# Folding the final weight into the experts' second weights, and weighing each expert's result where it is made

## The reference

```python
# x: 4096 tokens of 256 numbers; 8 experts, hidden size 512, 2 experts for each token
x = layernorm(x + attention(x))
gating = softmax(x @ Wg + bg)                       # 8 gates for each token
top = argsort(gating)[..., -2:]
h = silu((x @ W1[e] + b1[e]) * (x @ W3[e] + b3[e])) # for each expert e
expert = h @ W2[e] + b2[e]                          # 256 numbers
mixed = sum over the two chosen e of gating[e] * expert[e]
out = layernorm(x + mixed @ Wf + bf)
```

## Time and profile before

| | |
|---|---|
| median of 3 runs | 1953.55 us (1951.57 to 1959.17) |
| the profiled execution | 1948.98 us |
| its span in the trace | 1947.3 us |
| busy: PE / DVE / ACT / POOL | 89% / 65% / 45% / 19% of the span |
| granted TensorE clock, mean | 0.941 of full |
| moved by DMA | 155.30 MB, mean 80 GB/s |

### The profile page before, as it was taken

One profiled execution on the slowest core, in us unless ns is written; L12 is line 12 of the kernel. 1 busy time (PEld: TensorE's weight loads), 2 busy tenths in 40 slices (PEclk: granted clock), 3 DMA queues, 4 the chain that ended last, 5 costly groups with the idle time before them and its releaser, 6 DMA issues.

```text
span 1947.3 us, 28314 instructions
## 1 busy us (share of the span) xinstructions
PE 1737.1 (89%) x9130; PEld 920.4 (47%) x9131; DVE 1262.3 (65%) x2992; ACT 882.6 (45%) x1035; POOL 366.4 (19%) x478
## 2 busy tenths in 40 slices
...
GB/s 102 137 238 236 179 129 147 7 36 70 8 73 39 15 90 7 57 50 7 99 12 39 67 7 121 13 60 204 205 95 38 47 43 48 44 43 49 44 132 151
DMA packets 99497, 155.30 MB, mean 80 GB/s; under 512 B 10752, under 2 KB 60736, under 8 KB 99008
## 3 DMA queue, kind: packets, MB, share of 16 engines
...
## 4 chain that ended last, share of the span: by engine, by line
PE 70%; DVE 8%; ACT 7%; issue 6%; DMA 5%; POOL 2%; SPq 1%; another core or an unknown queue 0%; ACTq 0%; DVEq 0%; POOLq 0%
PE att_ps_s L884 22%; PE exp_ps_h L1564 13%; PE att_ps_o L903 12%; PE att_ps_m L862 10%; PE exp_ps_y L1582 6%; ACT att_probs L931 3%; DMA out_parts<-att_out_t 2%; PE pre_ps_q L311 2%; PE exp_ps_t L1572 2%; PE pre_ps_h L311 1%; DVE att_maxima L945 1%; DMA k_parts<-pre_waves 1%; PE exp_ps_x L1553 1%; POOL sorted_rows L1449 1%; DMA route_a_inv<-inv_rows 1%
## 5 line engine op out<-in xcount | busy, mean ns | idle before, releaser
L931 ACT ACTIVATE att_probs<-att_ps_s 128x1024 f32<-128x1024 f32 (+3 forms) x640 | 563.7, 895 | 484.4 <-PE att_ps_s L884 476.5
L884 PE MATMUL att_ps_s<-att_queries,att_keys 49*128 49x512 f32 (+3 forms) x2560 | 632.8, 561 | 20.9 <-ACT att_probs L931 11.4
L945 DVE TENSOR_REDUCE att_maxima<-att_ps_m 128x1 f32<-128x512 f32 x768 | 487.1, 684 | 153.6 <-PE att_ps_m L862 148.6
L862 PE MATMUL att_ps_m<-att_keys,att_queries 48*128 48x512 f32 (+3 forms) x1280 | 506.5, 605 | 24.1 <-DVE att_maxima L948 15.9
L862 PEld LDWEIGHTS att_ps_m<-att_keys,att_queries 48*128 48x128 f32 x1280 | 197.7, 193 | 315.8 <-DVE att_maxima L945 141.4
L884 PEld LDWEIGHTS att_ps_s<-att_queries,att_keys 49*128 49x128 f32 x2560 | 242.9, 191 | 127.3 <-ACT att_probs L931 85.4
L948 DVE CUSTOM_DVE_ANT_0 att_ps_m<-att_ps_m,att_future 128x128 f32<-128x128 f32 (+3 forms) x512 | 240.3, 514 | 73.4 <-PE att_ps_m L862 72.1
L903 PE MATMUL att_ps_o<-att_probs,att_values 128*32 128x512 f32 (+3 forms) x2560 | 269.3, 535 | 11.1 <-POOL att_probs L1034 11.1
L1564 PE MATMUL exp_ps_h<-keep_w,exp_rows_t 128*128 x568 | 257.4, 596 | 5.5 <-DVE exp_rows_t L1598 5.5
L1640 ACT ACTIVATE exp_hidden<-exp_product 128x512 f32<-128x512 f32 x71 | 44.8, 632 | 343.7 <-DVE exp_product L1623 343.7
L1034 POOL TENSOR_SCALAR_AFFINE_SELECT att_probs<-att_probs 128x512 f32<-128x512 f32 x128 | 81.1, 634 | 491.3 <-ACT att_probs L931 491.2
...
## 6 DMA issues: line engine op xcount, KB each, us to landing
...
```

The lines of the kernel that those rows point to most:

```text
L862: pe.matmul(take()[:, 0:width], queries[g % 2][half, c, r, P * q:P * q + P], keys[g % 2][half, k, r, 0:width], start=True, stop=True).then ...
L884: mm = pe.matmul(score_tile(unit, first, last)[:, e], keys[g % 2][half, k // TPC, r, P * (k % TPC):P * (k % TPC) + P].bitcast(F32), querie ...
L931: act.activation(probs[:, step % PROBS, DUO * r:DUO * r + DUO, first:last], score_tile(unit, first, last), ACT.Exp, scale=SCALE).then_inc( ...
L945: dve.tensor_reduce(to, buf[:, 0:width], AX.X, ALU.max).then_inc(s_mr, 1)
```

## The change

Since (g1 E1 + g2 E2) Wf = g1 (E1 Wf) + g2 (E2 Wf), the final weight can go into the experts' second weights. The kernel after does this:

1. In `route` the ten blocks of `bias2` (2) and `w2` (8), each 4 experts wide, are multiplied by Wf and put back in their place: PE transposes a block (`turn_weight`, 8 transposes, through the same `ps_n` as turn_x1), ACT copies it to `turned`, PE multiplies it by `wf` (`multiply_weight`, 8 matmuls of 256 columns into a new `ps_f`), ACT copies the product back (`keep_folded`). Four of these folds (`FOLDS_AMONG`) stand among the rounds of the chunks, six behind the last round.
2. `wf` is loaded in `route` (round 2). The `w2` blocks are loaded in rounds 1 to 4 and half of b1 in round 5. The other half of b1 has its place where `turned` lies, so SP waits for the last fold's multiplication before it loads it; SP's loads of the first sorted rows stand behind that.
3. A sorted row carries its two gates and the number of its first result row (260 numbers in place of 258). In `experts`, DVE finds the gate of a row in one more tiny instruction per tile, ACT multiplies each result by its gate (`weigh`), and POOL's scatter waits for that. The results of one token now lie in neighbouring rows.
4. `finish` has no mixing, transposing, copying or Wf: PE adds the two results of a token by multiplying each by the identity into the same PSUM tile (8 matmuls per chunk), and then come residual, statistics and norm as before. `picked` and `ps_y` have four buffers, `res` and `normed` two as before; the first chunk is loaded and the last one stored in halves. The order on DVE is residual(i), scale_and_shift(i-1); on ACT root(i), normalise(i-1).

The core of the diff:

```diff
...
+        folds = [(bias2[:, e:e + TPC], attended.s_bias, attended.bias_loads) for e in range(0, NE, TPC)]
+        folds += [(w2[:, k, e:e + TPC], s_w2[k], 16) for k in range(HK) for e in range(0, NE, TPC)]
...
+                if i == 2:
+                    for j in range(2):
+                        sp.wait_ge(attended.s_store[j], 32 * CHUNKS // 2)
+                        sp.wait_ge(attended.s_kept[j], 16 * CHUNKS // 2)
+                    sp.dma_start(wf[:, :], Wf.rearrange("(k p) n -> p k n", p=P)).then_inc(s_wf, 16)
+                if 1 <= i <= HK:
+                    to, rows = weight_blocks(w2, W2)[i - 1]
+                    sp.dma_start(to, rows).then_inc(s_w2[i - 1], 16)
+                if i == HK + 1:
+                    sp.dma_start(flat(bias1[:, TPC:NE]), flat_rows(b1[TPC:NE]).partition_broadcast(P)).then_inc(s_b1, 16)
...
+            sp.wait_ge(s_fm, len(folds))
+            sp.dma_start(flat(bias1[:, 0:TPC]), flat_rows(b1[0:TPC]).partition_broadcast(P)).then_inc(s_b1, 16)
...
+                if i >= 2:
+                    pe.wait_ge(s_ft, min(i - 1, FOLDS_AMONG))
                 turn_rows(pe, ps_n, x1[:, i * TPC:i * TPC + TPC, 0:D], ident[:, :]).then_inc(s_np, 1)
...
+            def turn_weight(j, p):
+                rows, loaded, count = folds[j]
+                pe.wait_ge(loaded, count)
+                pe.wait_ge(s_nt, min(j + 2, NCH))
+                if j >= 1:
+                    pe.wait_ge(s_ft, j)
+                turn_rows(pe, ps_n, rows, ident[:, :]).then_inc(s_fp, 1)
+
+            def multiply_weight(j, p):
+                if j == 0:
+                    pe.wait_ge(s_wf, 16)
+                pe.wait_ge(s_ft, j + 1)
+                if j >= 1:
+                    pe.wait_ge(s_folded, j)
+                multiply_rows(pe, ps_f, turned[:, p], wf).then_inc(s_fm, 1)
+
+            def among(f):
+                return lambda j, p: f(j, p) if j < FOLDS_AMONG else None
+            pipelined(pe, NCH, [(project, 1), (among(multiply_weight), 4), (turn_x1, 2), (count_before, 3), (project_gates, 2),
+                                (among(turn_weight), 3)], unrolled=True)
+            pipelined(pe, len(folds) - FOLDS_AMONG,
+                      [(lambda j, p: turn_weight(j + FOLDS_AMONG, (j + FOLDS_AMONG) % 2), 0),
+                       (lambda j, p: multiply_weight(j + FOLDS_AMONG, (j + FOLDS_AMONG) % 2), 1)], unrolled=True)
...
+            def keep_turned(j, p):
+                act.wait_ge(s_fp, j + 1)
+                if j >= 2:
+                    act.wait_ge(s_fm, j - 1)
+                act.copy(turned[:, p], ps_n[:, :]).then_inc(s_ft, 1)
+
+            def keep_folded(j, p):
+                act.wait_ge(s_fm, j + 1)
+                act.copy(folds[j][0], ps_f[:, :]).then_inc(s_folded, 1)
...
-                (exponential, 2)])
+                (exponential, 2),
+                (among(keep_turned), 3),
+                (among(keep_folded), 4)], unrolled=True)
+            pipelined(act, len(folds) - FOLDS_AMONG,
+                      [(lambda j, p: keep_turned(j + FOLDS_AMONG, (j + FOLDS_AMONG) % 2), 0),
+                       (lambda j, p: keep_folded(j + FOLDS_AMONG, (j + FOLDS_AMONG) % 2), 1)], unrolled=True)
...
+                if not since(s, 1):
+                    pe.wait_ge(routed.s_folded, routed.folds)
...
+                dve.scalar_tensor_tensor(gate[:, mine], rows[:, p, FIRST_WEIGHT:FIRST_WEIGHT + 1], is_first[:, mine],
+                                         rows[:, p, SECOND_WEIGHT:SECOND_WEIGHT + 1], ALU.mult, ALU.max).then_inc(s_gate, 1)
+                dve.scalar_tensor_tensor(dest[:, mine], rows[:, p, FIRST_ROW:FIRST_ROW + 1], is_first[:, mine], column(own_places),
+                                         ALU.subtract, ALU.min).then_inc(s_dest, 1)
...
+                if not since(s, 1):
+                    dve.wait_ge(routed.s_b1, 32)
...
-            pipelined(act, SLOT_TILES, [(activate, 1), (keep_hidden, 2)], body=4)
+
+            def weigh(s, p):
+                act.wait_ge(s_r, s + 1)
+                act.wait_ge(s_gate, s + 1)
+                act.activation(result[:, p], result[:, p], ACT.Copy, scale=gate[:, p:p + 1]).then_inc(s_gated, 1)
+            pipelined(act, SLOT_TILES, [(activate, 1), (keep_hidden, 2), (weigh, 3)], body=4)
...
-                pool.wait_ge(s_r, s + 1)
+                pool.wait_ge(s_gated, s + 1)
...
+        picked = n.sb(room, "picked", [P, 4, TPC, TOPK, D])
         res = n.sb(room, "res", [P, 2, TPC, D])
...
+        shift = n.sb(room, "shift", [P, 2, TPC])
+        norm = Norm(n, room, depth=2)
+        ps_y = [n.ps(f"ps_y{p}", [P, TPC, D]) for p in range(4)]
...
+        rows_in = expert_rows[0:TOPK * T].rearrange("(c t p r) d -> c p t r d", p=P, t=TPC, r=TOPK)
+        half = TPC // 2
...
-            sp.dma_start(wf[:, :], Wf.rearrange("(k p) n -> p k n", p=P)).then_inc(s_w, 16)
-
-            def load(i, p):
-                if since(i, 2):
-                    sp.wait_ge(s_mix, (i - 1) * TPC)
-                for r in range(TOPK):
-                    sp.dma_start(picked[:, p, r], at(rows_in[r], i)).then_inc(s_pick[p], 16)
-            pipelined(sp, NCH, [(load, 0)])
+            sp.dma_start(picked[:, 0, 0:half], rows_in[0][:, 0:half]).then_inc(s_begin, 16)
+            sp.dma_start(picked[:, 0, half:TPC], rows_in[0][:, half:TPC]).then_inc(s_pick[0], 16)
+            for i in range(1, NCH):
+                if i >= 4:
+                    sp.wait_ge(s_y, (i - 3) * TPC)
+                sp.dma_start(picked[:, i % 4], rows_in[i]).then_inc(s_pick[i % 4], 16)
...
+            for i in range(NCH):
+                parts = [slice(0, TPC)] if i < NCH - 1 else [slice(0, half), slice(half, TPC)]
+                for part in parts:
+                    pool.wait_ge(norm.s_done, i * TPC + part.stop)
+                    pool.dma_start(rows_out[i][:, part], normed[:, i % 2, part]).then_inc(s_out[i % 2], 16)
...
-
-            def turn(i, p):
-                pe.wait_ge(s_mix, i * TPC + TPC)
-                if since(i, 1):
-                    pe.wait_ge(s_mt, i)
-                turn_rows(pe, ps_m, mixed[:, p], ident[:, :]).then_inc(s_mp, 1)
-
-            def project(i, p):
-                pe.wait_ge(s_mt, i + 1)
-                if since(i, 2):
-                    pe.wait_ge(s_res, i - 1)
-                multiply_rows(pe, ps_y[p], mixed_t[:, p], wf).then_inc(s_y, 1)
-            pipelined(pe, NCH, [(turn, 0), (project, 1)])
+            for i in range(NCH):
+                if i >= 4:
+                    pe.wait_ge(s_res, i - 3)
+                for t in range(TPC):
+                    if i == 0 and t == 0:
+                        pe.wait_ge(s_begin, 16)
+                    elif t == (half if i == 0 else 0):
+                        pe.wait_ge(s_pick[i % 4], 16 * (i // 4 + 1))
+                    for r in range(TOPK):
+                        mm = pe.matmul(ps_y[i % 4][:, t], ident[:, :], picked[:, i % 4, t, r], start=(r == 0), stop=(r == TOPK - 1))
+                    mm.then_inc(s_y, 1)
 
...
-            def keep_mixed(i, p):
-                act.wait_ge(s_mp, i + 1)
-                if since(i, 2):
-                    act.wait_ge(s_y, i - 1)
-                act.copy(mixed_t[:, p], ps_m[:, :]).then_inc(s_mt, 1)
-            pipelined(act, NCH, [(normalise, 4), (weigh_first, 0), (keep_mixed, 1), (lambda i, p: norm.root(act, i, eps[:, 0:1]), 3)])
+                    act.activation(normed[:, p, t], res[:, p, t], ACT.Identity, scale=norm.rstd[:, p, t:t + 1],
+                                   bias=shift[:, p, t:t + 1]).then_inc(norm.s_done, 1)
+            pipelined(act, NCH, [(lambda i, p: norm.root(act, i, eps[:, 0:1]), 0), (normalise, 1)], unrolled=True)
...
-            def mix(i, p):
-                dve.wait_ge(s_pick[p], 16 * TOPK * ((i >> 1) + 1))
-                for t in range(TPC):
-                    dve.wait_ge(s_first, i * TPC + (t + 1))
-                    dve.scalar_tensor_tensor(mixed[:, p, t], picked[:, p, 1, t], gate(1, i, t), mixed[:, p, t],
-                                             ALU.mult, ALU.add).then_inc(s_mix, 1)
-
             def residual(i, p):
-                dve.wait_ge(s_y, i + 1)
-                if since(i, 2):
+                dve.wait_ge(s_y, i * TPC + TPC)
+                if i >= 2:
                     dve.wait_ge(norm.s_done, (i - 1) * TPC)
-                dve.tensor_tensor(res[:, p], ps_y[p][:, :], x1[:, i * TPC:i * TPC + TPC, 0:D], ALU.add).then_inc(s_res, 1)
+                dve.tensor_tensor(res[:, p], ps_y[i % 4][:, :], x1[:, i * TPC:i * TPC + TPC, 0:D], ALU.add).then_inc(s_res, 1)
                 dve.wait_ge(s_res, i + 1)
                 norm.statistics(dve, i, res[:, p])
 
             def scale_and_shift(i, p):
-                norm.scale_and_shift(dve, i, shift, s_shift)
-            pipelined(dve, NCH, [(mix, 0), (scale_and_shift, 3), (residual, 2)])
+                norm.scale_and_shift(dve, i, shift[:, p], s_shift)
```

(1 more changed line is left out.)

172 lines of the change are left out of this document (79 added, 93 removed).

## The result

The changed kernel takes 1967.49 us (median of 8 runs, 1963.45 to 1971.34) against 1955.53 for the kernel before beside it (8 runs, 1947.21 to 1959.17): ratio 1.0063, 95% interval 1.0042 to 1.0083, so slower by 0.6%. On a second chip the ratio was 1.0082 (1.0064 to 1.0100). The profiled execution took 1966.94 us, span 1965.2; the forecast was 1968.

What follows compares the result with a forecast made beforehand. PE bounds `experts`, a chain through the engines the rounds, DVE `finish`; +5 +16.5 -1.5 +0.5 -3.5 gave +17.0 us: 1966.0 from the profiled execution, 1970.5 from the median, forecast 1968, range 1952 to 1984.

Steps and rivals of the forecast that it cites:

- The folds among the rounds: Rounds of `route`: four folds add 10 us of PE work, 5 comes back by the clock, sum +5 us.
- I count 1.25 us back in each of four rounds: Rounds of `route`: busier PE raises its clock for the gates, 5 us back in all.
- The cover: Rounds of `route`: PE's wait ahead of the transposes of x1 hides 2.5 us of each fold.
- The rival of the full clock: Rounds of `route`: they fall by 8.7 us instead of rising by 5, +3.3 in all, 1955; chance 0.14.
- rounds on average under 13 us: Rounds of `route`: a listed sign that the forecast is wrong.
- The six folds behind: Between rounds and experts: the pause of 22 us hides two thirds of them; the experts start 16.5 us later.
- The experts' start: First tiles of `experts`: POOL's sums of bf end before DVE's work and no longer slow its product, -1.5 us.
- Equal clocks at the start: First tile of `experts`: PE idle before it in both kernels, so both taken to start at the low clock.
- Tiles: Steady tiles of `experts`: PE stays the bound at 5.82 us a tile, 0 us of change.
- The tail: End of `experts`: the last result passes ACT before its scatter, +0.5 us.
- `finish` with the tail: End stage: residual 0 8.3 us earlier, residuals 5.8 apart +4.1, last chunk +1.7, halved store -0.5; -3.0 us.
- the rival at PE's: `finish`: the wait does not stop DVE, period 3.62 us, 14.8 us less, +2.2 in all, 1954; chance 0.11 alone.

Runs made afterwards that it cites:

- e3: The changed kernel with all ten folds behind the rounds (FOLDS_AMONG 0 for 4): 1984.2 us, ratio 1.0158 to the kernel before.
- Experiment 1: The changed kernel with b1's first half loaded without waiting for the six late folds: ratio 1.0055 to the kernel before, 1.0019 when run again.
- e7: The changed kernel with six folds among the rounds, b1's first half freed of the late folds, `res` four times, `normed` three times: 1933.88 us, ratio 0.9912 to before.
- e2: The changed kernel with `res`, `shift` and the norm's moments held four times instead of twice in the end stage: ratio 1.0007 to the kernel before.
- second pair: Second traces of both kernels, unchanged: first projection at 1312.07 in the kernel before, 1315.46 in the changed kernel; ratio 1.0082.
- e5: The kernel before, unchanged, for a second trace: first projection at 1312.07, six rounds in 77.25 us.
- e6: The kernel before with only the changed kernel's placing of loads in the rounds, no folds: ratio 0.9988, six rounds in 76.2 us.

## Why the prediction came out

The forecast for the profiled execution was 1966.0 and it took 1966.9, but part of that is luck: two misses of 8 us cancel.

1. **The folds among the rounds: +5 forecast; the stage fell by 3.3.** The term that was mis-sized. The folds' own work was nearly right, 4.7 us each for 5.15. The step that failed is "I count 1.25 us back in each of four rounds", 5 in all, for the clock: everything else on PE became 9.5 us shorter against e3 and 11.2 against the first trace, since the projections gained too (24.60 us for 28.00 and 29.67), where the prediction counted the gates alone. The cover, PE's waits, counted as 10 us from two rounds of one trace, was 7.3 and 12.9. Against e3 that leaves +2.2 in the six rounds, under half of the 5. That the stage fell instead comes of what it is compared with, a slow draw: 122.2 us where three others without folds took 116.3 to 117.3. The rival of the full clock came nearest in the first trace, and its mechanism is there in part (0.84 instead of 0.72), but the rounds without folds were faster still at 0.74. The sign "rounds on average under 13 us", listed as one of being wrong, is there: 12.8.
2. **The six folds behind: +16.5 forecast, +17.3.** Right, by its own steps: a multiplication that straddles the rise of the clock (4.5 forecast, 5.19), then 4.7 each (4.88), bias and rows in one queue. The first transposes came 5.05 us behind the tenth multiplication, 5.5 forecast: the rows' load took 3.85 us, where I had taken 4.3, between 2.09 alone and 5.1 fully behind the bias. Experiment 1 took that away and e3 priced each fold at 4.8 us. The prediction let the experts start at the low clock in both kernels and so had the effect, but not its price: without the pause the first projection takes 2.3 us less.
3. **The experts' start: -1.5 forecast, -0.8.** Two products had met POOL's sums before (1.20 and 1.82 us), and both took 0.69, as said: -1.64. The first projection, at the low clock for longer, took 6.00 us for 5.19 and gave half of it back. Equal clocks at the start were the wrong part. e7 showed the opposite case.
4. **Tiles: 0 and 5.82 us each, exact.** The tail +0.5: last result to last scatter 1.79 us against 1.26.
5. **`finish` with the tail: -3.0 forecast (+0.5 and -3.5 in its sum), -3.5 measured** (-8.5 to residual 0 with the tail in it, against -8.3; +4.0 against +4.1; +1.0 against +1.2). The mechanism, residual(i) waiting for the normalising of chunk i-2 behind the shift just issued, shows as 2.21 us of idle DVE in each chunk, and e2, which took only the reason for the wait away, brought the period from 5.83 to 3.53 us. Once this wait is gone `finish` runs at DVE's pace, a little faster than in the rival at PE's.
6. **What the sum did not hold: +8.2 us ahead of the change.** In three traces without the change the first projection began at 1304.8 to 1312.1, in eleven with it at 1307.6 to 1319.0. The second pair differs by 3.4 us. The medians leave little room for a lasting part: stages behind it give +9.7 and +14.3 us in the two pairs, the medians +12 and +14. Yet the means of the first projection are 6 us apart, 1308.0 of three and 1314.0 of eleven, with single traces spread over 7 and 11 us. A lasting shift of an us or two stays open, and so does its reason.

DVE began on the gates 1 to 3.5 us after PE had ended them in four, two and one rounds of the three traces of the kernel before and its variant, and in none of the eleven others. In four of these seven `divide`, ahead of the gates in DVE's list, had itself begun late: in e5 twice and in e6 once it waited for the attention's rows (2.74, 4.00 and 3.23 us), and in the first trace once for 3.18 us without a named cause, after rows that had landed 12.68 us after their issue, behind b1. The other three, all in the first trace, stay open.
